# Banded attention with its q, k, v projections in three split terms, and head weights split in the first batch and streamed from scratch

## The reference, cut to what matters

```python
h = layernorm(x)                       # x: (4, 512, 512)
q, k, v = h @ wq.T, h @ wk.T, h @ wv.T # 16 query heads, 4 key and value heads, head width 128
q, k = rope(q), rope(k)                # halves swapped, times sin, plus the unswapped times cos
p = softmax(q @ k.T / sqrt(128))       # only keys at most 128 rows back, and none ahead
x = x + (p @ v) @ wo.T
```

## Time and profile before

| | |
|---|---|
| median of 3 runs | 2406.33 us (2403.66 to 2410.31) |
| profiled execution | 2406.55 us, span 2404.8 us |
| PE busy | 2151.0 us, 89% |
| DVE busy | 1712.6 us, 71% |
| POOL, ACT busy | 1048.7 us, 944.7 us |
| the stage's scores start, the next stage starts on DVE | 60.95 us, 928.67 us |

### The profile page before, as it was taken

One profiled execution on the slowest core, in us unless ns is written; L12 is line 12 of the kernel. 1 busy time (PEld: TensorE's weight loads), 2 busy tenths in 40 slices (PEclk: granted clock), 3 DMA queues, 4 the chain that ended last, 5 costly groups with the idle time before them and its releaser, 6 DMA issues. The chain is left out here.

```text
span 2404.8 us, 24923 instructions
## 1 busy us (share of the span) xinstructions
PE 2151.0 (89%) x7344; PEld 1108.7 (46%) x7344; DVE 1712.6 (71%) x2983; ACT 944.7 (39%) x1808; POOL 1048.7 (44%) x798
## 2 busy tenths in 40 slices
PE   6998999899999977997889898999789999999858
PEld 2554445454455543443555555465333433334234
DVE  1787788768876885786889889889546364654554
ACT  1443344333333433764655646465123232332311
POOL 2343354333333440322899998999511011010142
PEclk9999999999999998998999999999889999999979
DMA  7000000000000002455644526353332122221121
GB/s 263 19 19 18 19 20 20 18 18 22 22 18 19 23 23 90 159 186 214 266 162 166 197 105 210 127 203 108 107 80 78 41 77 57 70 70 46 52 109 53
DMA packets 95563, 214.87 MB, mean 89 GB/s; under 512 B 15832, under 2 KB 33112, under 8 KB 93032
## 3 DMA queue, kind: packets, MB, share of 16 engines
q1 hardware_dynamic: 77192, 156.18, 19.8%
q10 hardware_dynamic: 17760, 57.42, 6.7%
q0 software_dynamic: 512, 0.13, 0.0%
HBM read 146.30 MB, written 42.07 MB: 78 GB/s over the span
## 5 line engine op out<-in xcount | busy, mean ns | idle before, releaser
L759 POOL TENSOR_SCALAR a_prob<-a_prob,a_rsum 128x256 f32<-128x256 f32 x256 | 146.6, 590 | 467.3 <-DVE a_rsum L687 467.1
L1455 POOL TENSOR_TENSOR s_state<-s_b_rows,s_delta_u 128x1024 f32<-128x1024 f32 x128 | 303.5, 2384 | 36.9 <-DMA s_b_rows<-scan_bc 34.4
L1499 DVE TENSOR_TENSOR_SCAN s_state<-s_decay,s_state 128x512 f32<-128x512 f32 x256 | 304.9, 1211 | 15.5 <-ACT s_decay L1441 13.2
L1614 PE MATMUL c_bank<-c_xn_parts,c_w_parts 128*128 128x512 f32 (+1 forms) x1056 | 269.5, 405 | 6.2 <-DMA c_w_parts<-ffn_weights_lo 6.2
L1441 ACT ACTIVATE s_decay<-s_delta,s_a 128x512 f32<-128x512 f32 x256 | 173.5, 689 | 226.1 <-DVE s_state L1499 220.6
L491 PE MATMUL a_bank<-a_xn_t,a_wq 128*128 128x512 f32 x512 | 227.3, 592 | 0.0
L602 ACT ACTIVATE a_prob<-a_score,a_neg_m 128x256 f32<-128x256 f32 x256 | 117.6, 475 | 279.0 <-DVE a_neg_m L682 278.8
L1614 PEld LDWEIGHTS c_bank<-c_xn_parts,c_w_parts 128*128 128x128 f32 (+1 forms) x1056 | 196.3, 187 | 65.8 <-issue 20.3
L574 PE MATMUL a_bank<-a_wo,a_out_t 128*128 128x512 f32 x512 | 222.3, 593 | 0.0
L2049 ACT ACTIVATE d_prob_t<-d_score 128x512 f32<-128x512 f32 x256 | 138.9, 595 | 192.2 <-PE d_score L1931 191.1
L373 DVE TENSOR_SCALAR f_picks<-f_mask,f_lut_xor,f_lut 128x260 int32<-128x260 int32 x512 | 202.3, 468 | 9.6 <-DVE f_mask L367 0.5
(11 more groups left out here) (210 smaller groups left out, 3646.2 us busy)
## 6 DMA issues: line engine op xcount, KB each, us to landing
s_b_rows<-scan_bc SPq DMA_DIRECT2D x64, 512.0 KB, 3.7
c_w_parts<-ffn_weights_hi ACTq DMA_DIRECT2D x39, 512.0 KB, 3.6
c_w_parts<-ffn_weights_lo ACTq DMA_DIRECT2D x39, 512.0 KB, 4.5
f_idx<-in_idx SPq DMA_DIRECT2D x64, 130.0 KB, 2.1
ffn_weights<-f_picks SPq DMA_DIRECT2D x64, 130.0 KB, 1.8
d_qs<-d_hi SPq DMA_DIRECT2D x128, 64.0 KB, 2.0
d_ks<-d_hi SPq DMA_DIRECT2D x128, 64.0 KB, 2.0
d_factor<-in_factors SPq DMA_DIRECT2D x16, 512.0 KB, 3.6
```

Of the source, the lines that this page charges most:

```text
L1455: pool.tensor_tensor(self.state[:, s], row.broadcast_to([P, 2, T]), self.delta_u[:, h % 2], ALU.mult) \
L1499: dve.tensor_tensor_scan(self.state[:, s, e, :], self.decay[u % 2][:], self.state[:, s, e, :], 0.0, ALU.mult, ALU.add).then_inc(self.scann ...
L1614: mm = nc.tensor.matmul(banks[b][0:width[o], :], w_parts[:, n % SLOTS, w, at:at + width[o]], xn_parts[:, x_, k, :], start=((k, w, x_) == t ...
```

## The change

What it does:

- **Three terms.** Weights and normalised rows are split into a rounded part (f32r) and the remainder. A projection step is now twelve f32r matmuls 128x128x512 (high by high, low by high, high by low) in place of four in f32, for k, q and v. Scores, turns, p times v and wo stay as they were.
- **Splitting.** For the weights ACT rounds and POOL subtracts, in pieces of 128x512 (256 KB) through two raw buffers. Group 0's five pieces and v's four are done at the start, group 1's five ahead of the loop, groups 2 and 3 within groups 0 and 1 of batch 0. Each split group is stored to scratch. From group 2 of batch 0 on SP loads the parts (512 KB a step) from scratch. For the normalised rows ACT rounds all four tiles and DVE subtracts, where each copied two.
- **Loads.** wo (4 MB) and x's batches 1 to 3 (3 MB) go from ACT's queue to SP's, ahead of the first indices. Indices of chunk 1 of a group are loaded after the steps' weight loads, each of which waits for PE to finish that step of the next group.
- **Order.** Scores of heads 2 and 3 stand together after k and q0. In group 3 scores of all heads and the turn of the normalised rows stand ahead of the projections. DVE's adds to x stand between halves of the lookup, with the last `choose` behind them.

```diff
+class HeadWeights:
+    def load_piece(self, sp, m, source):
+        if m >= 2:
+            sp.wait_ge(self.split, m - 1)
+        sp.dma_start(self.raw[:, m % 2, :], source).then_inc(self.raw_in[m % 2], 16)
+    def load_raw(self, sp, n, p):
+        if n:
+            sp.wait_ge(self.stored[p], 16 * n)
+        self.load_piece(sp, self.piece(n, p), self.dram["head_w"][:, n * self.STEPS + p, :])
+    def subtract(self, pool, n, steps):
+        for p in steps:
+            m = self.piece(n, p)
+            pool.wait_ge(self.rounded, m + 1)
+            self.nc.gpsimd.tensor_tensor(self.parts[:, p, 1, :], self.raw[:, m % 2, :],
+                                         self.parts[:, p, 0, :].bitcast(F32), ALU.subtract) \
+                .then_inc(self.ready[p], 16)
...
@@ sync
+            heads.store(sp, 0)
+            for p, step in enumerate(proj(0)):
+                consumed(first, 0, step)
+                heads.load_raw(sp, 1, p)
+            sp.dma_start(wo[:], dram["wo_t"].rearrange("(h p) o -> p h o", p=P)).then_inc(w_in["wo"], 16)
+            for b in range(1, B):
+                sp.dma_start(x[:, b], dram["x"][b].rearrange("(t p) d -> p t d", p=P)).then_inc(x_in, 16)
+            def one_pass(i, more):
+                for g in range(KV):
+                    lookup.sync(sp, i, [g * TT])
+                    if first_pass and g + 1 < KV:
+                        heads.store(sp, g + 1)
+                    if not last_pass or g + 2 < KV:
+                        for p, step in enumerate(proj((g + 1) % KV)):
+                            consumed(ring, i, step)
+                            if first_pass and p == REPS:
+                                lookup.sync(sp, i, [g * TT + 1])
+                            if first_pass and g + 2 < KV:
+                                heads.load_raw(sp, g + 2, p)
+                            else:
+                                heads.load_parts(sp, (g + 2) % KV, p, ...)
+                    lookup.sync(sp, i, range(g * TT + (2 if first_pass else 1), (g + 1) * TT))
@@ tensor
+            def in_terms(bank, weights_of, xn_of):
+                for n, (wp, xp) in enumerate(TERMS):
+                    for k in range(KD):
+                        mm = nc.tensor.matmul(bank, weights_of(wp, k), xn_of(xp, k), ...)
...
@@ scalar
+            heads.round(act, 0, (0, 1))
             features(first, 0)
-            swap(first, 0, 0, 0, proj(0)[0:2])
-            load_queries(act, 1)
-            act.dma_start(wo[:], ...)
...
+            heads.round(act, 0, (2, 3, 4))
+            for k in range(KD):
+                heads.round_piece(act, heads.STEPS + k, wv[:, 0, k, :])
+                swap(first, 0, 0, 0, proj(0)[k:k + 1])
+            swap(first, 0, 0, 0, proj(0)[KD:])
             values(first, 0)
+            heads.round(act, 1, range(heads.STEPS))
             passes(act, one_pass)
```

More of the change, by code:

```diff
@@ L467, in _, with consumed @@
         def _(sp):
-            sp.dma_start(wk[:], dram["wk_t"].rearrange("(k p) o -> p k o", p=P)).then_inc(w_in["wk"], 16)
+            def consumed(ring, in_pass, step):
+                b, turn = ring.at(step, in_pass)
+                sp.wait_ge(ring.full[b], turn)
+            for p in range(heads.STEPS):
+                heads.load_raw(sp, 0, p)
             sp.dma_start(cos2[:], dram["cos2"]).then_inc(w_in["rope"], 16)
             sp.dma_start(sin2[:], dram["sin2"]).then_inc(w_in["rope"], 16)
-            load_queries(sp, 0)
@@ L476, in _ @@
+            passes(sp, one_pass)
             lookup.sync_end(sp)
@@ L618, in features @@
             def features(ring, i):
-                for k in (1, 3):
-                    take(("xn", k), i, xn_t[:, k, :], ring)
+                for k in range(KD):
+                    b, turn = ring.at(("xn", k), i)
+                    act.wait_ge(ring.full[b], turn)
+                    nc.scalar.copy(xn_t[:, 0, k, :], banks[b][:]).then_inc(xn_rounded, 1)
             def values(ring, i):
@@ L706, in one_pass @@
                     maxima(i, h + 1)
-                    inverse(i, h)
-                    lookup.pick(i, g * TT)
-                    rope(*at, nxt[0:2])
-                    maxima(i, h + 2)
-                    inverse(i, h + 1)
+                    if ng == 0 and more:
+                        inverse(i, h)
+                        features(ring, i, i + 1)
+                        maxima(i, h + 2)
+                        inverse(i, h + 1)
+                        maxima(i, h + 3)
+                        lookup.pick(i, g * TT)
+                        inverse(i, h + 2)
+                        rope(*at, nxt[0:2])
+                    else:
+                        inverse(i, h)
+                        lookup.pick(i, g * TT)
+                        rope(*at, nxt[0:2])
+                        maxima(i, h + 2)
+                        inverse(i, h + 1)
+                        maxima(i, h + 3)
+                        inverse(i, h + 2)
                     rope(*at, nxt[2:3])
-                    maxima(i, h + 3)
-                    inverse(i, h + 2)
                     lookup.choose(i, g * TT)
```

251 lines of the change are left out of this document (165 added, 86 removed).

## The result

| | before | after |
|---|---|---|
| median of 4 runs | 2407.49 us | 2475.31 us (2470.56 to 2478.97) |
| profiled execution | 2406.55 us | 2470.56 us |
| PE busy, DVE busy | 2151.0, 1712.6 us | 2119.4, 1745.9 us |
| PE's waits for POOL's probabilities | 20.6 us, 15 times | 114.5 us, 16 times |

The ratio is 1.0282, interval 1.0257 to 1.0306. The forecast was 2422: the sign was right, and the size was 64 us by the profiled executions (68 by the ratio) where 16 were expected.

A forecast was written before the change was run, and what follows sets the result against it. It took the path through DVE's lookup and POOL's product to bound a group, with PE's projections beside it. Batch 0 +15.6, batches 1 and 2 -5.4, batch 3 +6 on 2406.55 gave 2422 us, range 2397 to 2435.

The forecast's parts named there:

- Scores' start: Start of batch 0: scores begin at about 52 us instead of 60.95, with bounds of 48 to 58.
- Term 1: PE's projections: f32r matmuls 0.234 us apart, so 0.62 us less a step, 60 us of PE's work over 96 steps.
- Term 7: Stage's end: a 3.0 us choose and its store follow the last add, +5; batch 3 +6 to +7.
- Chunk 1's indices late by 5 us: Groups 0 and 1 of batch 0: masks of chunk 1 come 5 us late, behind the fourth raw piece.
- Term 6: Batch 0: first indices wait behind wo and x until 79.5; group 1 starts +15.0 late, batch 0 ends +15.6.
- Term 2: Groups 0 to 2: same path in groups 1 and 2, turn still 23.3 us after DVE's first maximum; group 2 gains 2.1.
- Term 3: PE's clock after waits in groups 1, 2 and 3: 1.4 us each time, +1.3 for group 1.
- Term 4: Group 3 of batches 0 to 2: 64.1 us to the next scores instead of 65.4; batches 1 and 2 together -5.4.
- D to D in groups 1 of batches 1 to 3 still 49 to 52 us: Time from DVE's first maximum in group 1 to that of the next group stays at 49 to 52 us.
- three things that I had named as showing the prediction wrong: Turn under 23 us after DVE's first maximum, first pick before 70 us, or groups below 48 us.
- rival (b): Batch 0's first indices don't wait in the queue; the pick starts 16 us sooner, sum 2406 us; chance 0.2.
- rival (c): Splitting in groups 0 and 1: ACT's waits for raw pieces add 5 us each, with cold clock 2436; chance 0.12.

The follow-up runs named there:

- e3: Changed kernel with only the first of three terms, four matmuls a projection step instead of twelve: 2438.5 us, ratio 1.0125.
- e4: Changed kernel with 20 bf16 matmuls on PE ahead of its wait for the probabilities, results overwritten: 2453.4 us, ratio 1.0169.
- e7: Kernel before with the change's scores' order, heads 2 and 3 together, on all engines, in group 3 too: 2432.2 us, ratio 1.0095.
- e5: Changed kernel with the scores' order of before for heads 2 and 3 in groups 0 to 2, on all engines: 2447.1 us, ratio 1.0151.
- e17: Changed kernel with POOL's sums of q1 moved behind the product of head 3's probabilities: 2477.4 us, ratio 1.0285.
- e1: Changed kernel with each choose right behind its pick and the last adds to x at the group's end, as before: 2450.3 us, ratio 1.0161.
- e2: Changed kernel with the first chunk of indices loaded right behind the table, ahead of raw pieces, wo and x: 2468.1 us, ratio 1.0240.
- e18: Changed kernel with loads moved, adds' and scores' orders of before, 12 matmuls ahead of the turn, and group 1's later pieces split later: 2414.6 us, ratio 1.0020.
- e13: Changed kernel with loads moved, adds' and scores' orders of before, and chunk 3's predicated copies 8 columns wide instead of 260: 2406.1 us, ratio 0.9992.

## Why the prediction was right or wrong

**Right.** Scores' start: 52 forecast, 52.9 measured. Matmuls 0.239 apart for 0.234 (Term 1). A choose behind the last add and +5 at the stage's end (Term 7): batch 3 is 17.2 longer, groups 0 to 2 make 12.2 of it. Chunk 1's indices late by 5 us: 5.52 in group 0 of batch 0. PE's waits over 60 us: 114.5. The transfers of parts at no cost. And the main reading, that the path of a group is DVE's and POOL's, with PE beside it, as far as PE's projections go (e3). What PE does behind the turn is not beside it: DVE waits 40.5 us for wo's tiles in the changed kernel, and a faster stretch from turn to wo gives 27 us (e4).

The sum missed by 48 us. 14 of them are in batch 0 with the start (+29.3 for +15.6, Term 6), 19 in batches 1 and 2 (+13.6 for -5.4, Terms 2 to 4), 11 in batch 3 (+17.2 for +6, Terms 2 and 3), and 4 in the part that nobody edited. The sign "D to D in groups 1 of batches 1 to 3 still 49 to 52 us" failed: they take 54.4, 53.9 and 54.6. None of the three things that I had named as showing the prediction wrong happened: all three watched for groups that are too fast, and it failed on the slow side.

**Wrong, Term 2**: "It is the same sum, D+21.1. The turn stays at D+23.3." It was D+22.3 and D+25.0. The count of instructions was right; the first choose was taken at the duration it had in the kernel before, and the new order put it beside POOL's sums of q1. The earlier trace rows showed the same thing for masks, and I used it for those alone. The order is worth 23 us on the kernel before (e7, 8 of them in group 3) and 32 on the changed one (e5; 19 in the profiled stage). e17 shows what lengthens the choose. How the 32 us split between the later inverse and what follows from that (the cold turn, the choose behind wo) is not shown.

**Wrong, Term 3**: 1.4 us per cold turn, and 1.9 less the slack for the choose behind the add. A cold turn cost 2.75 in group 1 of batch 1 (e4), and every turn was cold, in group 0 too, which I had counted half. With the turn 1.7 us later besides, DVE waited for wo's last tile in groups 0 to 2, and the choose stood behind that wait. So the last choose behind the last add cost 29 us in the changed kernel (e1; 15 in the profiled stage), where I let it cost 1.3 us in eight or so groups and 5 at the end.

**Wrong, Term 4**: group 3's turn at D+30.1 (508.24, D = 478.18) for 28.4, and 66.7 us from D to the next batch's scores for 64.1. Its choose takes 5.77 us beside POOL's sums, the same error:

```profile
499.90 5.77 DVE L383 COPY_PREDICATED f_picks<-f_mask,f_picks 128x260 int32<-128x260 int32 x7
```

**Mis-sized, Term 6**: batch 0's group 1 starts 22.1 us late, not 15.0. The mechanism, wo and x ahead in SP's queue, was right, and the first mask at 83.98 for 79.5 bears it out; rival (b) is out. 4.5 of the missing 7.1 us are at that mask. The other 2.6 come behind it, where the first choose takes 4.91 us and the turn is cold, as in every group; I haven't separated them. Group 1 is 8.0 longer for 4.0. I also followed only the indices through the queue. Group 2's raw pieces stand in it too, behind wo, x and the stores. That costs nothing on top in the changed kernel, but ACT waits for them once the indices are early (e2). Waits of ACT for raw pieces are rival (c), which I had at 0.12.

The change in all, by the ratios: 33 us from the queue, 32 from the scores' order, 29 from the adds' order, each undone alone, and 62 together; 6 us stay. In the profiled executions the next stage starts 19.0, 19.3 and 14.9 us earlier, 53 in all, and 50.6 with the three undone together. So whether the three overlap, as the ratios say, or add up, as the traces say, stays open.

## What to carry to other kernels

When an order is changed, give each moved or neighbouring instruction the duration it has beside its new neighbours, not its old one: here DVE's copies, and its masks too, took longer beside POOL's two-input sums, so look at what POOL runs in that stretch. When a transfer is put into a queue, walk through everything that stands behind it, not only the first thing that is wanted. If you put right one late load at a time, you may gain little, as the next late one takes its place (e2). And work taken from an engine that waits anyway makes its wait longer, and what comes behind the wait can run at the lower clock.

## What I had not expected of the hardware

Seven predicated copies of 128x260 took 2.98 us with POOL idle and 8.10 beside five of POOL's two-input sums. The slowdown goes the other way too: in e18 POOL's product of one head takes 1.88 us, and 3.21 where it stands beside a choose (80.16 to 83.33), which itself takes 3.17:

```profile
65.30 1.88 POOL L930 TENSOR_SCALAR a_prob<-a_prob,a_rsum 128x256 f32<-128x256 f32 x4 [0.66 <-POOL a_w_parts L454]
...
80.44 3.21 POOL L930 TENSOR_SCALAR a_prob<-a_prob,a_rsum 128x256 f32<-128x256 f32 x4 [0.31 <-DVE a_rsum L836]
```

After equal waits of PE (3.61 and 3.60 us, both in e13) twelve turns took 1.53 us in batch 1 and 2.82 in batch 2 (581.54 above):

```profile
363.34 1.53 PE L650 MATMUL a_bank<-ident,a_prob 128*128 128x128 f32 x12 [3.61 <-POOL a_prob L924]
```

The kernel before has the same: 2.82 us after the wait of 2.81 at 137.71, on which Term 3 rests, and 1.53 after 2.80 in the same group of batch 1. Twenty bf16 matmuls ahead of each wait, whose results nobody reads, made the changed kernel 27 us faster, and twelve of them nothing measurable once the three things were undone.
